# Convolution tap 8 of the small channel group: product by ScalarE, sum by GpSimd

## The reference

```
h = layernorm(x);  p = h @ w_in + b_in                 # 96 -> 192 channels
local = depthwise 3x3 convolution of p (SAME, 9 taps)
mixed = 0.25 * (four exponential scans of local) + local
x = x + layernorm(mixed) @ w_out + b_out
x = x + gelu(layernorm(x) @ w1 + b1) @ w2 + b2
```

## Time and profile before

| | us |
|---|---|
| median of 3 runs | 230.45 |
| lowest, highest | 229.41, 230.69 |
| profiled execution, its own time | 230.32 |
| its span, first to last instruction | 228.4 |
| PE busy | 219.6 (96%) |
| DVE busy | 182.7 (80%) |
| POOL busy | 148.8 (65%) |
| ACT busy | 137.0 (60%) |

### The profile page before, as it was taken

One profiled execution on the slowest core, in us unless ns is written; L12 is line 12 of the kernel. 1 busy time (PEld: TensorE's weight loads), 2 busy tenths in 40 slices (PEclk: granted clock), 3 DMA queues, 4 the chain that ended last, 5 costly groups with the idle time before them and its releaser, 6 DMA issues.

```text
span 228.4 us, 4138 instructions
## 1 busy us (share of the span) xinstructions
PE 219.6 (96%) x1332; PEld 182.3 (80%) x1332; DVE 182.7 (80%) x463; ACT 137.0 (60%) x308; POOL 148.8 (65%) x179
## 2 busy tenths in 40 slices
PE   8988896999999999999999999999999999999995
PEld 5676774889897989787888588888888878888885
DVE  7789999999999998996267987879696958667641
ACT  5765876768788675766563386636456552625262
POOL 7461877778979877949677573665849292836330
PEclk9999999999999999999999999999999999999999
DMA  3751000000000000000000003030313123021011
GB/s 110 214 178 54 1 0 0 4 0 0 3 0 1 3 1 0 3 0 0 0 3 0 1 36 106 34 105 0 117 58 118 56 83 93 34 70 37 0 40 63
DMA packets 11972, 9.30 MB, mean 41 GB/s; under 512 B 1232, under 2 KB 11696, under 8 KB 11952
## 3 DMA queue, kind: packets, MB, share of 16 engines
q1 hardware_dynamic: 11664, 8.97, 12.7%
q10 hardware_dynamic: 288, 0.09, 0.2%
HBM read 5.31 MB, written 3.74 MB: 40 GB/s over the span
## 4 chain that ended last, share of the span: by engine, by line
PE 80%; DVE 9%; DMA 4%; POOL 3%; issue 2%; SPq 1%; ACT 1%; DVEq 0%; POOLq 0%
PE bank L1410 12%; PE pA L1410 9%; PE pM L1361 8%; PE pM L1705 8%; PE bank L1535 7%; DMA x_all<-in_x 4%; DVE cA L1076 3%; PE bank L1578 2%; PE bank L1477 2%; PE bank L1583 2%; PE pA L1448 2%; PE bank L1680 2%; PE bank L1679 2%; PE bank L1685 2%; PE bank L1460 2%
## 5 line engine op out<-in xcount | busy, mean ns | idle before, releaser
L427 POOL TENSOR_TENSOR rs<-var,power 128x4 f32<-128x4 f32 x32 | 32.4, 1012 | 21.3 <-DVE var L967 18.2
L1076 DVE SCALAR_TENSOR_TENSOR cA<-pA,cols,cA 128x528 f32<-128x528 f32 x54 | 40.7, 754 | 0.2
L1361 PEld LDWEIGHTS pM<-w,hid 128*128 128x128 f32 x192 | 28.4, 191 | 5.7 <-issue 1.0
L1705 PEld LDWEIGHTS pM<-w,hid 128*128 128x128 f32 x168 | 26.9, 190 | 4.5
L1156 DVE SCALAR_TENSOR_TENSOR q<-th,bank 96x256 f32<-96x256 f32 x48 | 19.2, 412 | 13.3 <-PE bank L1410 13.3
L1361 PE MATMUL pM<-w,hid 128*128 128x96 f32 x192 | 28.9, 266 | 0.0
L1410 PE MATMUL pA<-q,a_half 96*96 96x256 f32 x96 | 27.0, 380 | 0.2 <-DVE q L1156 0.2
L1076 DVE SCALAR_TENSOR_TENSOR cB<-bank,cols,cB 128x256 f32<-128x256 f32 x56 | 26.4, 471 | 0.0
L1705 PE MATMUL pM<-w,hid 128*128 128x96 f32 x168 | 25.9, 266 | 0.0
L560 POOL TENSOR_TENSOR xl<-xt,xh 96x512 fp32r<-96x512 f32 x11 | 14.2, 1292 | 17.5 <-ACT xh L897 17.5
L1535 PE MATMUL bank<-local,mix 128*128 128x384 f32 x64 | 24.8, 497 | 0.1
(11 more groups left out here) (252 smaller groups left out, 612.7 us busy)
## 6 DMA issues: line engine op xcount, KB each, us to landing
moved<-blocks SPq DMA_DIRECT2D x11, 192.0 KB, 1.9
xt<-moved SPq DMA_DIRECT2D x33, 64.0 KB, 2.0
x_all<-in_x SPq DMA_DIRECT2D x8, 192.0 KB, 2.9
out<-y SPq DMA_DIRECT2D x7, 192.0 KB, 2.1
w<-in_w SPq DMA_DIRECT2D x1, 480.0 KB, 6.5
w<-in_w SPq DMA_DIRECT2D x1, 336.0 KB, 3.3
mix<-in_mix SPq DMA_DIRECT2D x1, 256.0 KB, 3.3
out<-y SPq DMA_DIRECT2D x2, 96.0 KB, 1.6
```

Source lines behind the costliest of these rows:

```text
L427: pool.tensor_tensor(rs[:, :], var[:, :], power[:, :], ALU.pow).then_inc(step, 1)
L1076: dve.scalar_tensor_tensor(out=acc, in0=src, scalar=col(f"k{'AB'[grp]}{k}"), in1=acc, op0=ALU.mult, op1=ALU.add).then_inc(s["conv_step"], 1)
L1361: last = pe.matmul(psum[:, k * D:(k + 1) * D], hid[:, j * TILE + k * P:j * TILE + (k + 1) * P], wc0("w2", j * D, (j + 1) * D), start=(j == ...
L1705: last = pe.matmul(dst, hid1[:, j * TILE + k * P:j * TILE + (k + 1) * P], wc1("m2", j * D, (j + 1) * D), start=j == 0 and (k == 0 if whole ...
```

## The change

Tap 8 of group B leaves DVE in tiles 1 to 7. ACT forms its product, a scaled copy of the shifted view of `pB`, into a new buffer `tap8` right behind tap 0 of group B. POOL adds `tap8` to `cB`, which then holds tap 0, between `rs2` and `xn2`. DVE's tap 1 of group B waits for that sum (`tap8_added`). DVE does taps 1 and 2 of group A ahead of taps 1 and 2 of group B. `conv_count` is adapted: 15 steps for a tile, and the last step of group B is tap 7, just ahead of tap 8 of group A.

```diff
@@ conv_count
-            return k if c == 0 else 16 * c - 8 + 2 * k - 1 + grp
+            order = {(1, 0): 1, (2, 0): 2, (1, 1): 3, (2, 1): 4, (8, 0): 15, (8, 1): 14}
+            return k if c == 0 else 15 * c - 7 + order.get((k, grp), 2 * k - 1 + grp)
@@ POOL, body0
                     minus_mean(ng2, st2, s["ln2_step"])
                     inverse_std(rs2, var2, s["ln2_step"])
+                if tile_known(f) and not peeled(f, 0):
+                    pool.wait_ge(s["tap0_done"], 2 * f + 2)
+                    pool.wait_ge(s["tap8_made"], f)
+                    pool.tensor_tensor(cB[f % 2][:, :], cB[f % 2][:, :], tap8[:, :], ALU.add).then_inc(s["tap8_added"], 1)
+                if tile_known(m):
                     wait(pool, s["tr2_done"], m)
                     pool.wait_ge(s["ln2_step"], 2 * m + 2)
-                if tile_known(m):
                     normalize(xn2, x2, ng2, rs2, s["xn2_ready"])
@@ ACT, first_taps
+                    if grp == 1:
+                        wait(act, s["tap8_added"], f - 1)
+                        act.activation(tap8[:, :].rearrange("c (r w) -> c r w", w=SIDE), tap_views(f, 8)[1][1], ACT.Copy,
+                                       scale=col("kB8")).then_inc(s["tap8_made"], 1)
@@ DVE, body0
                         if k == 1:
                             dve.wait_ge(s["tap0_done"], 2 * c + 1 + grp)
+                            if grp == 1:
+                                dve.wait_ge(s["tap8_added"], c)
...
                 elif tile_known(n):
-                    ln1_stats(lambda grp: tap(1, [grp]))
+                    ln1_stats(lambda at: tap(1 + at, [0]))
                 else:
-                    tap(1)
-                tap(2)
+                    tap(1, [0])
+                    tap(2, [0])
+                if peeled(c, 0):
+                    tap(2)
+                else:
+                    tap(1, [1])
+                    tap(2, [1])
                 tap(3)
...
-                    tap(8)
+                    tap(8, [0])
@@ PE, ln3_transposes and gu of the second block's tile 0
-                        pe.wait_ge(s["conv_step"], conv_count(TILES - 1, 8, 1))
+                        pe.wait_ge(s["conv_step"], conv_count(TILES - 1, 8, 0))
```

More of the change, by code:

```diff
@@ L186, in build @@
         cB = [sb(f"cB{k}", TOKENS) for k in range(2)]
+        tap8 = sb("tap8", TOKENS)
         local = sb("local", 2 * 2 * INNER)
@@ L213, in build @@
             "x_even_loaded", "x_odd_loaded", "bn1_step", "var1_ready", "ln1_step", "xn1_ready", "trx_done", "x1_split", "x1_lo",
-            "p_psum", "tap0_done", "conv_step", "cT_done", "local_ready", "mix_done", "mixed_ready",
+            "p_psum", "tap8_made", "tap8_added", "tap0_done", "conv_step", "cT_done", "local_ready", "mix_done", "mixed_ready",
             "bnm_step", "varm_ready", "lnm_step", "mtr_done", "mc_ready", "wout_done", "xb_ready", "x2_ready",
```

## The result

| | before | after |
|---|---|---|
| median, us | 229.90 (10 runs) | 231.23 (10 runs) |
| lowest, highest | 229.03, 230.75 | 229.84, 232.47 |
| after / before, 95% interval | | 1.0064 (1.0041 to 1.0088) |
| profiled execution, its own time | 230.32 | 232.47 |
| its span | 228.4 | 229.8 |

The change makes the kernel about 1.5 us slower (0.0064 x 229.9), between 0.9 and 2.0; between the medians it is 1.3. The median lies 0.2 us from the 231.4 of the forecast; the ratio lies just above the 0.5% line, with its interval across it.

A forecast was written before the change was run, and what follows sets the result against it. PE was taken to bound the loop from turn 3 on. The removal and ACT's copies gave 0, delays of tap 8 reaching PE added 1.0 us: 230.32 to 231.3 profiled, median 231.4, range 229.9 to 232.7.

The forecast's parts named there:

- PE's pace and the removal: PE sets the loop's 12.41 us a turn from turn 3 on; taking seven B taps off DVE gives 0.
- w_in_b's earlier release has no waiter: In PE's order L1460 follows L1448, so releasing w_in_b earlier gains 0.
- ACT's product: Seven more ACT copies of 0.47 us ahead of the gelu, costing 0 to 0.06 us a turn; taken as 0.
- The sum's 0.73 us: POOL's 128x256 addition between `rs2` and `xn2` takes 0.73 us, making what follows 0.55 us later.
- Tile 6: DVE's B1 waits for POOL's sum, so A3 comes 0.89 us later; 0.85 used.
- 0.4 us of wait on DVE in front of taps 6 to 8: Late `rs1` and `xn1` delay `mixed`, so DVE's `stm` waits 0.4 us before those taps.
- the new order's 0.25: Dependent taps in a row on DVE cost 0.25 us a tile, inside the 0.4 us wait in tiles 2 to 5.
- The recursion over the turns: Tap 8 delays reach PE every second turn, less slack: 0.4, 0.4, 0.8, 0.8, 1.1, 1.05 us in turns 2 to 7.
- (b): Rival: PE is the bound and hides everything, nothing given and nothing taken, 230.4 us; chance 0.22.
- (c): Rival: POOL's sum takes 1.00 us and is late, so each stall grows by 0.27: +2.2, 232.6 us; chance 0.23.
- (a): The forecast's own case: mixed delays of DVE's taps reach PE, +1.0 us; chance 0.45.
- (d): Rival: PE's even pace is really DVE's, so removing taps makes it faster, 228.6 us, at best 227.6; chance 0.10.

The follow-up runs named there:

- left_out_old_order: The kernel before without tap 8 of group B in tiles 1 to 7 on any engine, DVE's order otherwise unchanged: 229.73 us, ratio 0.9986.
- warm_before: The kernel before with four throwaway matmuls on PE in the wait of turn 2: 229.50 us, ratio 0.9992.
- lag: The changed kernel with group A two taps ahead of group B (three in tile 6), A's tap 8 no longer last: 229.70 us, ratio 1.0004.
- lag_before: The kernel before with group A two taps ahead of group B throughout, all eight B taps on DVE: 230.39 us, ratio 1.0019.
- pool_extra: The kernel before with an unused 128x256 addition on POOL between `rs2` and `xn2` in turns 1 to 6: 230.16 us, ratio 1.0007.
- sum_early: The changed kernel with POOL's sum moved ahead of its wait for `var2`, so ahead of `rs2`: 232.38 us, ratio 1.0099 to the kernel before.
- warm_after: The changed kernel with four throwaway matmuls on PE in the wait of turn 2: 230.37 us, ratio 1.0027 to the kernel before.
- order_alone: The kernel before with only DVE's new tap order; tap 8 of group B stays on DVE: 230.86 us, ratio 1.0046.
- tap_left_out: The changed kernel with tap 8 of group B left out on every engine in tiles 1 to 7, new order kept: 230.90 us, ratio 1.0039.
- spaced: The changed kernel with group A two taps ahead of group B throughout, tap 8 of A still last: 231.03 us, ratio 1.0049.

## Why the prediction came out as it did

**The total.** +1.0 forecast, +1.3 between the medians, +1.5 by the ratio: inside the range. That it comes so near is partly luck. The delays of which the forecast is made leave 0.3 us where the clock stays up (seven executions) and 0.6 with the four matmuls; the rest of the loss is the fall of the clock in turn 2, for which the forecast has no term.

**PE's pace and the removal: right in the time.** A distance of 12.40 to 12.42 us comes back in `left_out_old_order`, `warm_before`, `lag` and `lag_before`, whatever DVE does, and leaving the tap out altogether gives a ratio of 0.9986 (0.9960 to 1.0013). The freed time went where the prediction put it, into x2's wait. One statement is wrong for turn 1, "w_in_b's earlier release has no waiter": tile 1's group A lies in `pM`, so `w_in_a` waits for no tap of tile 1 there, and `w_in_b` is the one that waits for a tap. It costs no time by itself, but it matters for the clock, below.

**ACT's product: right.** 0.47 us (80.23), the gelu at 80.63 without a wait, and no wait of PE's behind it.

**The sum's 0.73 us: right** to the last digit shown, by the line between two other widths. The delay of `xn1` was 0.47 instead of 0.55. That the line between two widths was exact is luck in part: the same width took 0.61 us in `pool_extra`.

**Tile 6: right.** A3 follows A1 by 3.05 us (80.59 to 83.64), where it was 2.14: 0.91 against the 0.89 forecast. The stretch grew by 0.83; I used 0.85.

**The step that failed: "0.4 us of wait on DVE in front of taps 6 to 8", with the new order's 0.25 "inside" it.** It is the other way round. No `stm` waits for `mixed` in the changed kernel, and the addition on POOL alone changes nothing that can be told. The new order alone costs 1.0046 (1.0024 to 1.0067), and it alone gives the changed kernel's stretches outside tile 6. Its price was also mis-sized: A1 to A3 grew by 0.33 us and not 0.25 (the pair of A taps stands 1.62 - 0.76 = 0.86 apart in tile 5, where tile 0's row gave 0.80, and the pair of B taps 0.52; in tile 6 the A pair has 1.56 - 0.76 = 0.80 again. In tile 5 a wait for `st1`'s step stands between the two, in tile 6 none; no run takes it away), and the stretches grew by 0.37, 0.26, 0.31, 0.31 and 0.25 in tiles 2, 3, 4, 5 and 7. The stretches came out near the forecast's 0.4 because two delays that end at the same `stm` don't add, and the larger was near the one I had chosen; that is luck. The larger was the order's, since it lies on DVE itself, and the `mixed` that comes 0.47 later than x2 wants it finds DVE not there yet. `sum_early` shows what it takes to make the other one decide: 0.5 us more on POOL.

**What the Trainium skill says** (VectorE: DVE Perf Modes, "The DRAIN you can't avoid") is that eight copies took the same time with a semaphore after each as with one after the last. The forecast read more into it, that the new order would be free: all taps here have a semaphore, in both orders, and that sentence doesn't tell whether an instruction reads what the one ahead wrote. In these runs that is what goes with the cost: 0.80 to 0.86 us against 0.66 from start to start at 528 elements, and 0.52 against 0.39 at 256. Behind an A tap everything independent starts 0.66 to 0.68 later, a B tap, `varm` or a statistic alike; an independent A tap behind an A tap was not run.

**The recursion over the turns: right from turn 3 on.** The distances of the changed kernel exceed 12.41 by 0.30, 0.02, 0.24 in turns 4, 5, 6, and by -0.04 against 12.61 in turn 7; the forecast was 0.4, 0, 0.3 and -0.05. A delay of tap 8 enters every second turn, over x2 and w_out. In turn 3 the forecast was 0; against the 12.40 of the kernel before it was +0.19 where the clock had fallen and -0.07 in `warm_after`, where it had not.

**What wasn't foreseen: the clock in turn 2.** PE waits 2.09 us there instead of 1.53, and in 15 of 22 executions the clock then falls to its lower level until about 40 us. Two things together make the wait that long. One is the chain over POOL, `rs1` and `xn1`: ACT's `mixed` starts 7.51 us behind x2, where it was 6.95. The other is that PE gets to the wait early. Where tap 8 of group B is DVE's last tap, `w_in_b` of turn 1 waits for it, as in `pool_extra`:

```profile
28.21 0.39 PE L1464 MATMUL bank<-xh,wi_h 97*128 97x256 f32 x1 [0.80 <-DVE cB L1080]
```

In the changed kernel it doesn't, and PE starts its last work ahead of the wait (the scan matrix, L1552) 3.57 us behind x2, where in `pool_extra` it is 4.02. By kernel:

| | addition on POOL behind `rs2` | `w_in_b` of turn 1 waits | wait of turn 2 | executions with the fall |
|---|---|---|---|---|
| `order_alone` | no | 0.81 | 1.05 | 0 of 12 |
| `tap_left_out` | no | no | 1.50 | 0 of 12 |
| `left_out_old_order` | no | no | 1.53 | 1 of 12 |
| `pool_extra` | yes | 0.80 | 1.53 | 0 of 12 |
| `lag` | yes | 0.41 | 1.85 | 0 of 12 |
| `spaced` | yes | no | 2.08 | 8 of 12 |
| the change, both times | yes | no | 2.09 | 15 of 22 |

Either of the two alone leaves the wait at 1.5 us and the clock up, but for one execution; both together bring the fall. In the profile of the kernel before `w_in_b` happens not to wait (wait of turn 2: 1.53), in that of `warm_before` it waits 0.81. None of the kernel before's 99 executions beside the experiments shows the fall.

From the transposes of tile 0's sum (at 17.97 us before) to those of tile 7 it is 84.55 us before, 86.39 in the changed kernel, 85.54 with the four matmuls: 1.84 us lost, 0.85 of it with the clock. These are single executions, and the measure is good to some 0.5 us only: it is 85.00 in `warm_before`, whose time is that of the kernel before. I read the granted clock of the kernel before as 1.0 throughout and didn't ask what a longer wait would do to it. The term is worth 0.7 to 1.0 us on the median.

**The rivals.** (b), hidden altogether: refuted for the kernel as a whole by the interval, and for the taps by the 0.45 us of longer distances in `warm_after`; but with the clock up little of the time is left, so (b) was nearer than the total shows. (c), the sum late: not as put, since it takes 0.73 us, but the loss ended between (a)'s 1.0 and (c)'s 2.2. (d), DVE the pace: refuted by the kernel without the tap.

**Open.** What decides whether the clock falls isn't settled: after 2.08 us in `spaced` it stayed in the profiled execution, after 2.09 us in two others it fell, and after 1.03 to 1.85 us it stayed in all that were profiled, though one execution of `left_out_old_order` and one of `sum_early` (profiled waits 1.53 and 1.65) have a mean clock of 0.993. How the rest of the changed kernel's loss divides isn't settled either: why `order_alone` loses 1.0 us with the clock up and the changed kernel only 0.3 to 0.6. The changed kernel's profiled execution also begins 1 us earlier (tile 0's transposes are at 16.98), and in its second block ACT waits 14.9 us for DMA in all, 13.4 before; neither is part of a claim here.

## What to carry to other kernels

Work taken off an engine gives nothing where that engine already waits for the pace-setter behind it: find the wait that would swallow it, then ask what the move costs where it lands. Price a new order like a new instruction: an instruction put right behind the one whose output it reads cost 0.13 to 0.20 us each time here, and a kernel in which nothing but the order was changed lost 0.46%. Where two delays end at one point, take away each alone before naming the cause. When a change lengthens a wait of TensorE, look at the granted clock behind it, and compare the executions with and without a fall before sharing out the loss: here the fall was half of it or more.

## What the runs showed of the hardware

DVE's small `tensor_scalar` (128x4) is stretched when POOL's addition runs beside it. Three rows of the changed kernel: alone, on DVE,

```profile
42.61 0.17 DVE L977 TENSOR_SCALAR var<-st 128x4 f32<-128x4 f32 x1
```

and under a POOL addition of 1.02 us, DVE's row and then POOL's:

```profile
25.86 0.76 DVE L1142 TENSOR_SCALAR varm<-stm 128x4 f32<-128x4 f32 x1
```

```profile
25.57 1.02 POOL L440 TENSOR_TENSOR xb<-x_all,brow 128x384 f32<-128x384 f32 x1
```

It takes 0.17 us alone and 0.76 here, and ends (26.62) when POOL's addition ends (26.59). The same is seen in the 0.38 to 0.40 of `var2` under POOL's `x_all` in both kernels. The Trainium skill (SBUF — State Buffer, "Who interferes with whom") has `tensor_scalar` among the operations that can take the pair of ports shared with GpSimd, whoever comes second then waiting for the whole instruction; this agrees. The taps beside the same additions keep their 0.75 and 0.47 us. So a POOL instruction that is added to a kernel has a price on DVE even where nobody waits for its result: 0.05 to 0.21 us a tile in `pool_extra`, 0.19 of it read off `var1` in tile 5 (A2 starts 0.26 behind it, 0.07 before).

The granted clock fell to 0.50 (1.2 GHz) after a single wait of 2.09 us within an otherwise busy TensorE, for 3 to 4 us, in 15 of 22 executions, and four matmuls put into that wait kept it at 0.999 or more in 12 of 12.
